# Later rank counts and slot tables in the first expert layer of a two-layer decoder

## The reference

```
logits = h2 @ router_w                      # 8 experts
probs = softmax(logits)
topw, topi = top_k(probs, 2)
topw = softmax(topw)
combine = sum(one_hot(topi, 8) * topw[..., None], axis=1)
shared = swiglu(h2, sh_gate, sh_up, sh_down)            # d_ff = 512, every token
gate, up = h2 @ e_gate[e], h2 @ e_up[e]                 # for each expert e
eout[e] = (silu(gate) * up) @ e_down[e]
out = X + shared + sum_e combine[:, e] * eout[e]
```

## Time and profile before

| | us |
|---|---|
| median of 3 runs | 1553.23 (1552.87 to 1554.06) |
| the profiled execution, its own time | 1552.87 |
| span of that execution, first to last instruction | 1551.1 |
| around the span (1552.87 - 1551.1) | 1.8 |
| PE busy | 1338.0 (86% of the span) |
| DVE busy | 855.5 (55%) |
| ACT busy | 583.3 (38%) |
| POOL busy | 707.6 (46%) |
| mean granted TensorE clock | 0.932 of full speed |

### The profile page before, as it was taken

One profiled execution on the slowest core, in us unless ns is written; L12 is line 12 of the kernel. 1 busy time (PEld: TensorE's weight loads), 2 busy tenths in 40 slices (PEclk: granted clock), 3 DMA queues, 4 the chain that ended last, 5 costly groups with the idle time before them and its releaser, 6 DMA issues.

```text
span 1551.1 us, 33541 instructions
## 1 busy us (share of the span) xinstructions
PE 1338.0 (86%) x11888; PEld 1057.8 (68%) x11888; DVE 855.5 (55%) x1978; ACT 583.3 (38%) x1281; POOL 707.6 (46%) x954
## 2 busy tenths in 40 slices
PE   5999879979999999889899999289989999887950
PEld 3666648966777777668889999166656776666740
DVE  3787743337888888556212222567765665482423
ACT  2545526414444555542122221044434444323310
POOL 5456531026676566500233332167864554126526
PEclk9999969979999999889999999699999999877985
DMA  6000000020000000001788996500000000016964
GB/s 230 2 1 0 2 22 7 0 83 18 15 11 2 9 15 18 15 4 41 260 324 314 323 328 236 183 1 1 11 11 22 22 27 15 8 53 214 373 179 144
DMA packets 47079, 137.42 MB, mean 89 GB/s; under 512 B 6813, under 2 KB 29486, under 8 KB 40816
## 3 DMA queue, kind: packets, MB, share of 16 engines
q1 hardware_dynamic: 32656, 110.05, 20.1%
q0 software_dynamic: 7536, 19.67, 3.9%
q10 hardware_dynamic: 6768, 6.16, 1.1%
HBM read 119.21 MB, written 17.56 MB: 88 GB/s over the span
## 4 chain that ended last, share of the span: by engine, by line
PE 66%; DVE 11%; DMA 7%; issue 6%; POOL 5%; ACT 3%; SPq 0%; DVEq 0%; POOLq 0%; ACTq 0%
PE ps L937 9%; PE ps L886 8%; PE ps L1203 8%; PE ps L1078 8%; PE ps L985 5%; DMA row_in<-rows_of,from_u 4%; PE ps L963 4%; PE ps L1215 4%; PE ps L954 4%; PE ps L992 2%; PE ps L877 2%; PE ps L874 2%; DVE negmax L1644 2%; PE ps L912 2%; PE ps L853 2%
## 5 line engine op out<-in xcount | busy, mean ns | idle before, releaser
L1203 PE MATMUL ps<-hT,w_tile 128*128 128x128 f32 x1624 | 200.6, 279 | 7.2 <-DMA w_tile<-in_w_f 6.5
L1644 DVE TENSOR_REDUCE negmax<-ps 128x8 f32<-128x1024 f32 x128 | 156.0, 1219 | 88.4 <-PE ps L886 88.4
L1203 PEld LDWEIGHTS ps<-hT,w_tile 128*128 128x128 f32 x1624 | 191.9, 195 | 10.0 <-DMA w_tile<-in_w_f 7.9
L1272 ACT ACTIVATE probsT_all<-ps 128x1024 f32<-128x1024 f32 x128 | 131.2, 1025 | 174.8 <-PE ps L886 174.8
L886 PE MATMUL ps<-qe,kf 32*128 32x256 f32 x1280 | 154.1, 389 | 0.0
L886 PE MATMUL ps<-ke,qf 32*128 32x256 f32 x1024 | 144.3, 400 | 0.0
L626 POOL DMA_INDIRECT row_in<-rows_of,from_u x86 | 83.3, 969 | 123.1 <-DVE to_u L1986 73.4
L680 POOL TENSOR_SCALAR eps_sum<-mv 128x1 f32<-128x1 f32 x112 | 25.4, 227 | 219.1 <-DVE mv L1583 187.7
L886 PEld LDWEIGHTS ps<-qe,kf 32*128 32x128 f32 x1280 | 111.3, 190 | 5.2 <-issue 2.7
L985 PE MATMUL ps<-probsT_all,va 128*32 128x128 f32 x2560 | 105.3, 282 | 7.0 <-ACT probsT_all L1272 4.2
L2112 DVE TENSOR_TENSOR h_in<-ps,act_sb 128x512 f32<-128x512 f32 x39 | 27.0, 692 | 145.2 <-PE ps L1203 138.4
(11 more groups left out here) (263 smaller groups left out, 3294.6 us busy)
## 6 DMA issues: line engine op xcount, KB each, us to landing
w_tile<-in_w_f SPq DMA_DIRECT2D x39, 1536.0 KB
w_tile<-in_w_f SPq DMA_DIRECT2D x47, 385.0 KB
back_of<-w_odd ACTq DMA_DIRECT2D x47, 128.0 KB
ctxT<-in_ctxT SPq DMA_DIRECT2D x32, 128.0 KB, 2.0
rows_of<-nv SPq DMA_DIRECT2D x32, 128.0 KB, 1.7
y_back<-back_of SPq DMA_DIRECT2D x8, 512.0 KB, 4.9
w_even<-in_w_att SPq DMA_DIRECT2D x3, 1024.0 KB, 7.6
x_all<-in_x SPq DMA_DIRECT2D x4, 512.0 KB, 10.8
```

The source lines that it names most:

```text
L1203: last = mm(ps[:, 2 * which + at.two, fc * P:(fc + 1) * P], w[:, col:col + P], rowT[:, at.two, c, :], start=c == 0, stop=c == KC - 1)
L1272: nc.scalar.activation(half_of(probsT_all, half), ps[:, 2:4].rearrange("p b n -> p (b n)"), ACT.Exp, scale=HD ** -0.5).then_inc(S["probs"], 1)
L1644: nc.vector.tensor_reduce(m, ps[:, 0:2].rearrange("p b (h k) -> p (b h) k", h=HB), AX.X, ALU.max, negate=True).then_inc(S["s_max"], 1)
```

## The change

Three engines get another order of the same instructions; nothing is computed differently.

1. TensorE: `ranks` moves from ahead of up(2) to behind it, and the wait for `rank_sb`, which stood behind up(2), now stands at the end of `ranks` for both MoE parts (for MOE1 it stood there already, with the same value 4).
2. VectorE: slot pieces 0 and 1 move from the hooks of q = 8 and 9 to that of q = 11; pieces 2, 3 and 4 from q = 10, 11 and 12 to q = 12, 13 and 14. Piece 5 stays at q = 15.
3. ScalarE: `nth_of_slots` moves from the hook of q = 12 to that of q = 13.

```diff
--- before.py
+++ after.py
@@ -1118,11 +1118,9 @@
 
                 def body(e, p):
                     for g in range(GROUPS):
+                        up(e, p, g)
                         if f == MOE0 and g == 2:
                             ranks(units("acc_done", f, e, 0, GT))
-                        up(e, p, g)
-                        if f == MOE0 and g == 2:
-                            pe.wait_ge(S["rank_sb"], 2)
                         if g:
                             down(e, p, g - 1)
                         elif not (isinstance(e, int) and e == 0):
@@ -1163,8 +1161,7 @@
                     mm(out, tri_bf[:], chosen[:, FRONT:, 0:n], start=True, stop=False)
                     mm(out, ones_bf[:], sums[:, 1, FRONT - 1:FRONT - 1 + NT, 0:n], start=False, stop=True)
                     mm(ps[:, 5, D:D + n], ones_bf[:], sums[:, 1, FRONT + NT - 1, 0:n], start=True, stop=True).then_inc(S["rank_out"], 1)
-                    if f == MOE1:
-                        pe.wait_ge(S["rank_sb"], 4)
+                    pe.wait_ge(S["rank_sb"], 2 * (f - MLP))
 
                 experts(pe, f, body)
                 n_e = F_EXPERTS[f] - 1
@@ -1437,7 +1434,7 @@
                 if step_ == 4 and f == MOE0:
                     act.wait_ge(S["gate_p"], 2)
                     nc.scalar.activation(w12[:, :, 1:2], w12[:, :, 0:1], ACT.Exp).then_inc(S["act_gate"], 1)
-                if step_ == 12 and f == MOE0:
+                if step_ == 13 and f == MOE0:
                     nth_of_slots(f)
 
             def nth_of_slots(f):
@@ -2005,10 +2002,11 @@
                     link(ts(w12[:, :, 2], w12[:, :, 1], 1.0, None, ALU.add))
                     link(nc.vector.reciprocal(w12[:, :, 3], w12[:, :, 2]))
                     link(tt(w12[:, :, 2], w12[:, :, 1], w12[:, :, 3], ALU.mult))
-                if step_ in (8, 9, 10, 11, 12):
-                    slots(MOE0, step_ - 8)
-                if step_ == 15:
-                    slots(MOE0, 5)
+                if step_ == 11:
+                    slots(MOE0, 0)
+                    slots(MOE0, 1)
+                if step_ in (12, 13, 14, 15):
+                    slots(MOE0, step_ - 10)
 
             def gate_moe1(step_):
                 s4 = sc[:].rearrange("p t (g e) -> p (t g) e", g=4)
```

## The result

| | before | after |
|---|---|---|
| first comparison, median | 1553.23 us (7 runs) | 1562.69 us (7 runs), ratio 1.0065 [1.0039, 1.0092] |
| second comparison | 1554.65 us (35 runs) | 1560.96 us (12 runs), ratio 1.0027 [1.0005, 1.0050] |
| third comparison | 1553.85 us (35 runs) | 1559.41 us (12 runs), ratio 1.0025 [1.0010, 1.0040] |
| profiled execution: time, span | 1552.87, 1551.1 us | 1559.64, 1557.8 us |
| mean granted clock of it | 0.932 | 0.928 |

A forecast was written before the change was run, and what follows sets the result against it. TensorE was taken to set the pace in MOE0's shared expert. Profiled 1552.87 + 3.7 (waits and gains at full clock) + 1.5 (one clock fall) = 1558.1 us; with 0.36 for the median, 1558.4; range 1555.3 to 1561.0.

The forecast's parts named there:

- the clock's term: MOE0's shared expert: one fall of TensorE's granted clock behind the new waits, +1.5 us; chance 0.42.
- the chain: MOE0's shared expert, down(0) to down(3): gains and new waits at full clock sum to 3.69 us later.
- two or more falls: Rival: the clock falls behind both new wait clusters, 3.7 + 3.4 = +7.1 us, 1560.3 us; chance 0.16.
- Part 1: TensorE after down(0): up(2) starts 0.12 us behind its last matmul, without waiting for group 0's adds; 0.83 us gained.
- Part 2: Ahead of down(1): rank copies released from chunk 11's hook, new TensorE wait of some 2.5 us, net 1.96 us late.
- Part 3: Chunks 12 to 15: late pieces keep VectorE busy without break; second new TensorE wait, 2.4 us, ahead of `origins`.
- The smaller edits: ScalarE's `nth_of_slots` ahead of chunk 14's Silu is covered by 0.25 us; SyncE's later first routed-weight load is free.
- only the rank wait counts: Rival: VectorE ends the tables before down(2) ends, leaving at most +2.0 us, 1555.2 us; chance 0.06.
- absorbed: Rival: the routed tiles' waits for transfers eat the shared expert's delay, 1553.2 us; chance 0.06.
- faster: Rival: TensorE keeps the 0.83 and 0.66 us gains and no new wait replaces them, 1551.7 us; chance 0.05.

The follow-up runs named there:

- the fillers: Changed kernel plus ten idle matmuls in each of the two new TensorE waits, fp32r then bf16: 1557.93 us (ratio 1.0025) and 1557.16 us (1.0026).
- filler there: Kernel turned round plus ten idle bf16 matmuls ahead of chunk 6: 1554.04 us, ratio 0.9986 against the kernel before.
- the adds first: Changed kernel with the four adds of group 2 ahead of slot piece 5 on VectorE: 1557.09 us, ratio 1.0020 against the kernel before.
- only the late ranks: Changed kernel with pieces 1 to 3 in chunk 11's hook, piece 4 and ScalarE's product in chunk 12's: 1557.74 us, ratio 1.0016 against before.
- only the late tables: Kernel before with pieces 2, 3, 4 and ScalarE's product one or two hooks later, ranks unmoved: 1557.83 us, ratio 1.0023.
- without the rank wait: Changed kernel with rank counts in bank 0, so down(1) need not wait for the copies: 1557.59 us, ratio 1.0008 against the kernel before.
- the kernel turned round: Kernel before with ranks ahead of down(0), pieces 1 to 3 in hooks 8 to 10, group 2's adds ahead of piece 5: 1550.69 and 1552.24 us.

## Why the prediction was wrong

**What failed is the size of the clock's term.** The prediction's step reads "I take one fall", at 1.5 us. The runs showed two, 3.4 us in all: behind the rank wait and behind the wait for the tables, in each of the three profiles of the changed kernel. With the chain that is its rival "two or more falls", 3.7 + 3.4 = +7.1 us, and the stretch grew by 7.0. I had given it 16%. One fall was also mis-sized, at 1.5 us where the fillers give 1.7. The reason for the mistake is the one row that I let decide, the wait of 2.46 us (ahead of chunk 7) behind which the clock stayed up. The same wait is in 16 profiles without filler there, and the clock fell behind it in 13 of them: the row was the exception. The two new waits of 2.4 us, together or one alone, were followed by a fall 11 times out of 11: twice each in the three profiles of the changed kernel and in that with the adds first, once each with only the late ranks, only the late tables, and without the rank wait.

The Trainium skill (TensorE: Matmul & The Clock Gate, "HAM oscillation — how this bites in real kernels") warns only of waits longer than these. By that rule no fall would have come; the 11 falls out of 11 decide against it here.

**The range was too narrow as well.** It was made from the cases of the stretch alone. The three times of before that I had lay within 1.2 us, but 35 of them spread over 13 to 16 us. That puts the first median, 1562.69 us, outside, while the stretch itself asked for 1560.3. No run ties the other 2.4 us to the change: the two later medians, 1560.96 and 1559.41, do not repeat them. Nor is it a merit of the prediction that these two lie in its range, since its sum has one fall too few.

**What was right,** step by step:
- *Part 1:* forecast 0.83 us gained, up(2) 0.12 us behind down(0). Measured: 697.16 after 697.04, no wait.
- *Part 2:* forecast a new wait of some 2.5 us, down(1) 1.96 us late. Measured: 2.44 us, released by `n_all`; 1.83 us late.
- *Part 3:* forecast a second wait of 2.4 us, VectorE unbroken from chunk 12 with 3.08, 5.56, 5.56 us. Measured: 2.40 us, and 3.09, 5.55, 5.57. The stall of 0.66 us in chunk 15 is gone, as forecast.
- *The sum of the chain:* forecast 3.69 us. Measured with fillers, at full clock: 3.57 to 3.60.
- *The smaller edits:* ScalarE's product and Silu behind it were covered by 0.25 us in the forecast; in the timeline after, the Silu ends at 729.08 + 0.58 = 729.66 and VectorE takes it up at 729.89:

```profile
727.81 1.36 ACT L1262 ACTIVATE tile_in<-slot_tile,nth 128x1248 bf16<-128x1248 bf16 x1 [2.13 <-DVE slot_tile L1960]
729.08 0.58 ACT L1495 ACTIVATE act_sb<-ps 128x512 f32<-128x512 f32 x1
```

- *The rivals:* "only the rank wait counts" is excluded by the second wait; "absorbed" by the first routed tile, which follows the last add after 1.79 us as before, and by the second, with its wait for weights, after 8.96 us (9.03 before); "faster" by both waits.

**What stays open.** The stretch is 7.0 us longer, but the second and third comparison give +4.2 and +3.9 us for the whole by their ratios (6.3 and 5.6 by their medians), the third with an interval (1.6 to 6.2) that excludes 7.0, while the first gives +10.1. A part may be given back behind the stretch: from the last routed tile to the end there are 582.6, 583.3 and 584.3 us in the profiles of the changed kernel and 584.4, 585.9, 588.4 and 583.8 in those of before. With that scatter in either kernel, no run here settles it.

## What to carry to other kernels

When a result is drained from one bank while the next product waits, move the drain to where the draining engine has nothing in hand, not behind the last chunk of a group: there its whole chain lies bare (2.44 us here). Work that is needed only later should be spread over the groups in which its engine has slack. Pushed together behind the last start of the group, 13.9 us of cover (from chunk 12's `h_tmp` to the end of down(2)) met 16.3 us of work. And a new wait of the engine that sets the pace was paid twice here, once for its length (a chain of 3.6 us) and once for the clock behind it (3.4 us), so both belong in the sum; where one profile shows a random event once, that is one draw, not a rule.

## What the hardware showed that I had not expected

- Waits of TensorE of 2.40 to 2.47 us at full clock were followed by a low clock in 24 of 27 cases over all profiles (11 of 11 in the places of the change, 13 of 16 ahead of chunk 7), at a price of 1.6 and 1.9 us for the two in the first profile of the changed kernel; the 2.18 to 2.19 us wait ahead of down(3), where the clock was still up when it began, in only one of seven. Ten idle matmuls of 128x512 in the wait, 2.3 us (bf16) or 2.5 to 2.6 us (fp32r), kept the clock at 1.00 in all four waits so filled.
- Length alone doesn't decide it. A wait of 2.98 us in the second half of the launch, which all 17 profiles have at full clock, left the clock up in 7 of them and was followed by a fall in 10. In the first profile of the kernel before, from which I made the forecast, it left it up, and I had not counted that row. In the second profile of the kernel turned round even a wait of 3.85 us did. What decides, no run here shows. For each of the two, the timeline row and the window behind it:

```profile
1137.43 0.89 PE L963 MATMUL ps<-w_odd,oT 128*128 128x256 f32 x3 [2.98 <-issue]
1137.50:1140.90 3.40, 3.40 (x32) 1.00 0.00 0
```

```profile
749.15 1.05 PE L1207 MATMUL ps<-hT,w_tile 128*128 128x128 f32 x7 [3.85 <-DMA w_tile<-in_w_f]
749.20:752.60 3.40, 3.40 (x30) 1.00 0.99 423
```

- The stretch under study repeats to 0.02 us over four profiles of the kernel before, while the whole launch of the same kernel varies by 10 us among them.
